# Two experts' weights loaded when the slot table is known, and a shorter piece of each zeroed row written first

## The reference

```python
x = x + layernorm(rwkv_block(layernorm(x)))      # time mixing (scans), channel mixing
xf = layernorm(x).reshape(-1, 256)
shared = (gelu(xf @ w1s) * (xf @ w2s)) @ w3s     # 256 -> 1024 -> 256
idx = argmax(xf @ Wg, axis=-1)                   # one of 8 experts for each token
for e in range(8):
    y = (gelu(xf @ W1[e]) * (xf @ W2[e])) @ W3[e]
    final = final + where(idx == e, y, 0)
out = x + layernorm(shared + final)
```

## Time and profile before

| | us |
|---|---|
| median of 3 runs | 1000.21 |
| lowest, highest | 999.18, 1000.51 |
| the profiled execution | 1001.62 |
| its span | 999.7 |
| chunk phase, to the first up matmul of slot 0 | about 664 |
| slot phase | about 336 |

### The profile page before, as it was taken

The page is one execution under the profiler, slowest core; times in us unless marked ns, Lnnn a source line. Parts: engine busy times, 40 slices in busy tenths (PEclk is TensorE's granted clock), DMA queues, the critical chain, the costliest instruction groups (busy, mean ns, idle before and its releaser), DMA issues.

```text
span 999.7 us, 27993 instructions
## 1 busy us (share of the span) xinstructions
PE 924.4 (92%) x9734; PEld 836.7 (84%) x9734; DVE 725.1 (73%) x1651; ACT 586.2 (59%) x1014; POOL 591.2 (59%) x800
## 2 busy tenths in 40 slices
PE   2477999999999999999999999869999999999994
PEld 1366888888888889888888878769999999999994
DVE  6999999999999999999999985614444444444442
ACT  5487768868868868869778755313333333333340
POOL 5475766866866866866866441434455555555553
PEclk9699999999999999999999999989999999999998
DMA  7033152152253153163171263936787778576410
GB/s 240 13 107 112 48 212 79 71 212 70 81 212 105 42 218 97 42 221 94 42 254 53 86 211 128 336 132 188 232 273 250 232 250 273 171 245 216 159 56 21
DMA packets 82091, 152.09 MB, mean 152 GB/s; under 512 B 5423, under 2 KB 62896, under 8 KB 76914
## 3 DMA queue, kind: packets, MB, share of 16 engines
q1 hardware_dynamic: 34528, 72.39, 21.1%
q10 hardware_dynamic: 42944, 61.98, 19.2%
q0 software_dynamic: 4560, 16.98, 4.4%
HBM read 183.59 MB, written 46.25 MB: 230 GB/s over the span
## 4 chain that ended last, share of the span: by engine, by line
PE 64%; DVE 11%; POOL 8%; issue 7%; ACTq 4%; DMA 3%; ACT 3%; SPq 1%; POOLq 0%; DVEq 0%
PE up L366 12%; PE up L368 12%; PE up L367 12%; PE yp L366 6%; PE yp L368 6%; PE yp L367 6%; PE yp L572 2%; PE yp L575 2%; PE tp L375 2%; ACTq L940 2%; PE yp L588 2%; DVE arena L1026 2%; POOL mix_s L1608 1%; DVE er L1127 1%; POOL routed_rows L1641 1%
## 5 line engine op out<-in xcount | busy, mean ns | idle before, releaser
L366 PE MATMUL up<-mix_s,arena 128*128 128x128 f16 x1248 | 211.9, 219 | 0.3 <-DVE ex L1474 0.2
L367 PE MATMUL up<-mix_s,arena 128*128 128x128 f16 x1248 | 211.8, 219 | 0.0
L368 PE MATMUL up<-mix_s,arena 128*128 128x128 f16 x1248 | 211.8, 219 | 0.0
L366 PE MATMUL up<-xf_s,arena 128*128 128x256 f16 x512 | 139.5, 272 | 1.5 <-issue 1.5
L1707 POOL TENSOR_TENSOR kf_s<-ex,kf_s 128x512 f16<-128x512 f32 x78 | 90.2, 1156 | 85.6 <-ACT kf_s L986 85.5
L368 PE MATMUL up<-xf_s,arena 128*128 128x256 f16 x512 | 139.5, 273 | 0.0
L367 PE MATMUL up<-xf_s,arena 128*128 128x256 f16 x512 | 139.5, 272 | 0.0
L1474 DVE SCALAR_TENSOR_TENSOR ex<-up,ex 128x512 f32<-128x512 f32 x78 | 53.9, 691 | 102.6 <-ACT ex L980 102.5
L366 PEld LDWEIGHTS up<-mix_s,arena 128*128 128x128 f16 x1248 | 122.4, 98 | 1.3 <-DVE ex L1474 1.2
L367 PEld LDWEIGHTS up<-mix_s,arena 128*128 128x128 f16 x1248 | 122.4, 98 | 0.4
L368 PEld LDWEIGHTS up<-mix_s,arena 128*128 128x128 f16 x1248 | 122.4, 98 | 0.0
(11 more groups left out here) (226 smaller groups left out, 2865.6 us busy)
## 6 DMA issues: line engine op xcount, KB each, us to landing
arena<-w_split ACTq DMA_DIRECT2D x113, 1024.0 KB
arena<-in_W SPq DMA_DIRECT2D x24, 1024.0 KB, 6.5
w_split<-arena SPq DMA_DIRECT2D x24, 1024.0 KB, 9.2
rows<-routed_rows ACTq DMA_DIRECT2D x39, 261.0 KB, 2.8
arena<-w_split SPq DMA_DIRECT2D x9, 1024.0 KB
normed<-routed_rows ACTq DMA_DIRECT2D x37, 128.0 KB, 2.5
x_in<-in_x SPq DMA_DIRECT2D x16, 256.0 KB, 2.8
x_res<-in_x SPq DMA_DIRECT2D x16, 256.0 KB, 2.8
```

What stands on the lines that cost most here:

```text
L366: pe.matmul(out, stat(0), mov(0), start=first, stop=False)
L367: pe.matmul(out, stat(0), mov(1), start=False, stop=False)
L368: return pe.matmul(out, stat(1), mov(0), start=False, stop=last)
```

## The change

The prefetch is taken out. The up weights of slots 0 and 1 are loaded by SP once the table names their experts, slot 0's ahead of its x, and slot 1's between the two loads of x. The down piece of slot 0 is loaded by ACT, without a condition. Ahead of the first x only the last 260 numbers of each zeroed row are written (ID to ROW), for all 8 experts by SP; the first 520 follow after slot 1's x, under a semaphore of their own, which ACT waits for ahead of its first load of a slot's rest. ACT issues no zeros. The tile of zeros shrinks from 780 to 520 numbers.

```diff
@@ -120,7 +120,7 @@
         x2 = sb("x2", tok)
         gate_r = sb("gate_r", tok)
         relu_k = [sb(f"relu_k{b}", chan) for b in range(2)]
-        zero_row = ex.rearrange("p n k c -> p (n k c)")[:, 2 * CT * CH:2 * CT * CH + ROW]
+        zero_row = ex.rearrange("p n k c -> p (n k c)")[:, 2 * CT * CH:2 * CT * CH + ID]
         mixed2 = relu_k
         kf_s = sb("kf_s", [2, FT, CH], F16)
         kf = kf_s.rearrange("p h f n -> p (h f n)").bitcast(F32).rearrange("p (f n) -> p f n", f=FT)
@@ -296,9 +296,15 @@
 
                 sp.wait_ge(S("end_at"), 1)
                 sp.wait_ge(S("zero_row"), 1)
-                for e in range(E // 2):
+                for e in range(E):
                     at = sp.value_load(end_at[0:1, e:e + 1], min_val=0, max_val=E * REGION - P)
-                    sp.dma_start(routed_rows[bass.ds(at, P)], zero_row).then_inc(S("zeroed"), 16)
+                    sp.dma_start(routed_rows[bass.ds(at, P), ID:ROW], zero_row[:, 0:ROW - ID]).then_inc(S("zeroed"), 16)
+
+            def other_zeros_at_ends():
+
+                for e in range(E):
+                    at = sp.value_load(end_at[0:1, e:e + 1], min_val=0, max_val=E * REGION - P)
+                    sp.dma_start(routed_rows[bass.ds(at, P), 0:ID], zero_row).then_inc(S("zeroed_rest"), 16)
 
             def half(w, part):
                 return w.rearrange("p m h (k n) -> p (m h k) n", k=CT)[:, :, part * F // 2:(part + 1) * F // 2]
@@ -306,37 +312,24 @@
             def up_halves(e, part):
                 return half(w_split[bass.ds(e, 1), :, 0:2].rearrange("e p m h n -> (e p) m h n"), part)
 
-            def likely_slots():
-
-                sp.wait_ge(S("scattered1"), 16 * TT * (NC // 2 - 1))
+            def first_slots():
+
+                sp.wait_ge(S("slot_table"), 2)
                 for m in range(3):
                     sp.wait_ge(S(f"expert_lo{m}"), E)
-                    sp.wait_ge(S(f"expert_out{m}"), 16 * (E - 1))
-                for part in range(2):
-                    sp.dma_start(half(expert_w[0][:, 0:2], part),
-                                 half(w_split[0, :, 0:2], part)).then_inc(S(f"slot_w{part}_0"), 16)
-                sp.dma_start(expert_w[0][:, 2], w_split[0, :, 2]).then_inc(S("slot_w2_0"), 16)
-                for m in range(3):
                     sp.wait_ge(S(f"expert_out{m}"), 16 * E)
-                for part in range(2):
-                    sp.dma_start(half(expert_w[1][:, 0:2], part),
-                                 half(w_split[0, :, 0:2], part)).then_inc(S(f"slot_w{part}_1"), 16)
-
-            def first_slots():
-
-                sp.wait_ge(S("slot_table"), 2)
-                sp.wait_ge(S("scattered_xf"), 16 * TT)
-                sp.wait_ge(S("zeroed"), 16 * E)
-                for b in range(2):
-                    sp.wait_ge(S(f"scattered{b}"), 16 * TT * (NC // 2 - b))
                 for n in range(2):
+                    e = sp.value_load(slot_expert[0:1, n:n + 1], min_val=0, max_val=E - 1)
+                    for part in range(2):
+                        sp.dma_start(half(expert_w[n][:, 0:2], part),
+                                     up_halves(e, part)).then_inc(S(f"slot_w{part}_{n}"), 16)
+                    if n == 0:
+                        sp.wait_ge(S("scattered_xf"), 16 * TT)
+                        sp.wait_ge(S("zeroed"), 16 * E)
+                        for b in range(2):
+                            sp.wait_ge(S(f"scattered{b}"), 16 * TT * (NC // 2 - b))
                     at = sp.value_load(slot_row[0:1, n:n + 1], min_val=0, max_val=E * REGION - P)
                     sp.dma_start(slot_x[n], routed_rows[bass.ds(at, P), XF:XF + C]).then_inc(S(f"slot_x_in{n}"), 16)
-                    e = sp.value_load(slot_expert[0:1, n:n + 1], min_val=0, max_val=E - 1)
-                    for part in range(2):
-                        sp.wait_ge(S(f"slot_w{part}_{n}"), 16)
-                        sp.dma_start(half(expert_w[n][:, 0:2], part), up_halves(e, part),
-                                     cond=e != 0).then_inc(S(f"slot_w{part}_{n}"), 16)
 
             def step(i, p, h):
                 for part in range(2):
@@ -353,9 +346,9 @@
                 for e, m in early_piece(i, p, h) + last_late(i, p, h) + late_now(i, p, h):
                     store_expert(e, m)
                 if at_step(i, NC + 1):
-                    likely_slots()
                     zeros_at_ends()
                     first_slots()
+                    other_zeros_at_ends()
 
             chunk_steps(sp, step)
 
@@ -403,7 +396,7 @@
                 if is_slot(j):
                     wait(pe, S("slot_x_lo"), j + 1)
                     for q in range(2):
-                        wait(pe, S(f"slot_w{q}_{b}"), 16 * (h + 2))
+                        wait(pe, S(f"slot_w{q}_{b}"), 16 * (h + 1))
                         wait(pe, S("slot_g"), 2 * j + q - 1)
                         for m in range(2):
                             for g in range(FT // 2):
@@ -414,7 +407,7 @@
                                                lambda s: slot_xs[b][:, s, k, :], k == 0, k == CT - 1)
                         mm.then_inc(S("slot_up"), 1)
                 if is_slot(j - 1):
-                    wait(pe, S(f"slot_w2_{1 - b}"), 16 * (h + 2 * b))
+                    wait(pe, S(f"slot_w2_{1 - b}"), 16 * (h + b))
                     wait(pe, S("slot_h_lo"), 2 * j)
                     wait(pe, S("slot_sum"), j - 2)
                     if at_step(j, 2):
@@ -831,13 +824,6 @@
                     for n in own_pieces(OWN_HI, i, part):
                         own_hi(n)
 
-                def zeros_at_end(e):
-                    if at_step(i, NC + 1):
-                        act.wait_ge(S("end_at"), 1)
-                        act.wait_ge(S("zero_row"), 1)
-                        at = act.value_load(end_at[0:1, e:e + 1], min_val=0, max_val=E * REGION - P)
-                        act.dma_start(routed_rows[bass.ds(at, P)], zero_row).then_inc(S("zeroed"), 16)
-
                 def late_hi():
                     for e, m in late_piece(i, p, h):
                         expert_hi(e, m)
@@ -883,8 +869,6 @@
                 gelu(0)
                 if at_step(i, NC):
                     late_hi()
-                zeros_at_end(E // 2)
-                zeros_at_end(E // 2 + 1)
                 gelu(1)
                 if not at_step(i, -1):
                     ln0(i + 1, 1 - p)
@@ -904,8 +888,6 @@
                     early_hi()
                 mix_hi(0)
                 sh_hi(0)
-                zeros_at_end(E // 2 + 2)
-                zeros_at_end(E // 2 + 3)
                 if at_step(i, NC + 1):
                     gelu(2)
                 mix_hi(1)
@@ -949,9 +931,6 @@
                 fresh = None
                 if not isinstance(n, int) or n >= 2:
                     fresh = e != expert_of(n - 2)
-                if at_step(n, 0):
-                    act.wait_ge(S("slot_w2_0"), 16)
-                    fresh = e != 0
                 wait(act, S(used), value)
                 if part == 2:
                     dst, src = expert_w[b][:, 2], w_split[bass.ds(e, 1), :, 2]
@@ -988,6 +967,7 @@
                                        ACT.Copy).then_inc(S("slot_h_hi"), 1)
                     if at_step(j, 0):
                         act.wait_ge(S("scattered_rest"), 16 * TT * 2)
+                        act.wait_ge(S("zeroed_rest"), 16 * E)
                     at = rows_of(j)
                     wait(act, S("slot_done"), j - 1)
                     act.dma_start(slot_rest[b], routed_rows[at, 0:OFF + 1]).then_inc(S(f"slot_rest_in{b}"), 16)
```

## The result

Over five runs each the changed kernel took 1004.56 us (1002.68 to 1004.79) and the kernel before 999.18 (998.62 to 1000.51). The ratio is 1.0043, with a 95% interval of 1.0029 to 1.0058: slower by 4.3 us, 2.9 to 5.8 (the two medians lie 5.4 apart). The forecast was 1003.2, slower by 3.0, in a range of 1000.4 to 1006.8.

What follows compares the result with a forecast made beforehand. PE was taken to bound the kernel, so slot 0's start decides: +1.5 us for x of slot 1 and +1.5 for the clock make +3.0, 1003.2 us; the 8 in 10 range was 1000.4 to 1006.8.

Steps and rivals of the forecast that it cites:

- What bounds: PE bounds the slot phase, so time gained or lost at slot 0's first matmul reaches the end whole.
- Zeros: SP's eight short zeros before the first x take 1.12 us a turn, end at 648.1, land about 2.1 us after issue.
- the rival of SP's slow loop: SP's register reads stay slow, eight zero turns of 1.68 us end at 652.6: 1007.6 us in all, chance 0.15.
- Slot table and weights: Before slot 0: table ready at 648.2, first weight issue at 649.4, x issues near 651.6 and 656.
- x of slot 1: Behind weights in queue 1 it lands at 664.8; slot 0's matmuls start at 665.4 instead of 663.86, +1.5 us.
- Clock: PE's two gaps leave slot 0 at half speed for 4.7 us instead of 1.8, until 670.1: +1.5 us.
- The sum: Slot 0's later start and the low clock, 1.5 + 1.5 = +3.0 us, giving 1003.2 us.
- Costed at nothing: Slot 0's down weights and ACT's wait for the rest zeros add no time; the cover is 3 to 5 us.
- ACT held: Rest zeros landing as late as 678 delay ACT's gelu of slot 1 past its cover: 1005.2 us, chance 0.08.
- Faster: The x loads pass the weights in queue 1, slot 0 starts at 659.0: 994.4 us, chance 0.07.

Runs made afterwards that it cites:

- the two experiments that brought slot 0 forward: Changed kernel with x of slot 1 ahead of slot 1's weights: 1.0038; kernel before with short zeros first, prefetch kept: 0.9968.
- the other two with prefetch: Kernel before with short zeros first: 0.9968; the same plus slot 0's rest load by SP and both x issued together: 0.9975.

## Why the prediction was right, point by point

**What bounds.** Slot 0's start decides, and the rest follows: borne out by the kernels with moved orders only so far as ACT and DVE keep up. The changed kernel's delay of 2.5 us at that start and 2.9 at slot 0's end reached the end of its span as 3.1.

**Zeros.** Eight turns were to end at 648.1 and took until 648.7; the register read took 0.27 as taken, so the rival of SP's slow loop is out. The reason given was wrong, though: it put the slow reads of before down to the loaded queue, but the reads of the rest zeros, the first of them with some 2 MB ahead in SP's queue, took 0.28:

```profile
L306 SPq TENSOR_LOAD <-end_at x8: 266/277/684, 659.2 to 668.3; - x8
```

The short zeros landed 1.7 us after issue, 2.1 forecast.

**Slot table and weights.** The table was forecast for 648.2. Its last cast took 1.14 us and ended at 648.8; the first weight issue was at 649.78 (649.4 forecast). x of slot 0 was issued at 651.74 (651.6) and x of slot 1 at 656.46 (656).

**x of slot 1.** Landed near 665.7 against 664.8, and x of slot 0 near 659.3 against 657.6. The order in the queue was right. So was the rate: 4.46 MB of queue 1 from 650.7 to 664.2 are 0.33 MB/us, beside the other queues. SP's queue after, in 651 to 663, in 651 to 652 and in 659 to 665:

```profile
q1 hardware_dynamic: 3872, 3.90, 98.0%
```

```profile
q1 hardware_dynamic: 212, 0.22, 65.7%
```

```profile
q1 hardware_dynamic: 2029, 2.12, 109.0%
```

Without its first microsecond the first stretch holds 3.68 MB in 11 us, 0.335 MB/us, and the last ran at 0.353. What was mis-sized was the start. The first weights were issued 0.4 us late, and 0.22 MB are what 0.335 MB/us moves in 0.7 us, so the full rate counts from about 651.3 (an estimate from these rows) and not from 650.7. That is 0.6 of the 0.9 us by which x of slot 1 was late; the rest is not placed. The term came out at +2.5 instead of +1.5. The Trainium skill has two limits in "DMA: Bandwidth & Descriptors", section Specifications: queue 1 reaches the fabric's 435 GB/s in none of these stretches, and the 358 GB/s of HBM per core stand just above its best, 353. All queues together went beyond 358 where zeros were written beside the loads, with 399 GB/s in 666 to 667, so as a limit of everything that a core moves the trace does not bear it out.

**Clock.** Forecast +1.5; measured +0.4 in both profiles of the changed kernel and +1.7 in that of the kernel with only the rest load moved, which has the same passage. It was low at slot 0's start, as said. The forecast had it rise 5.2 us after PE's second start, as before after the only one; it rose after 3.0 and 3.1 us in the first two, so that slot 0 ran slow for 2.6 us instead of 4.7, and after 5.8 us in the third. What decides this is open, so the size of this term was within what occurs but could not be had from the one profile of before. The forecast also knows of no fall ahead of the gaps. The page "TensorE: Matmul & The Clock Gate" of the Trainium skill, section HAM oscillation, has each wait paid anew; the low clock at slot 0's start agrees with it (0.50 in 666 to 667), but the extra price in this case was 0.4 us twice and 1.7 once.

**The sum** of 3.0 met 2.9 at slot 0's end because one term was 1.0 too small and the other 1.1 too large: that is luck, and with the clock of the third profile the measured sum would have been 4.2. The measured 4.3 (2.9 to 5.8) is somewhat more; what the remainder is made of is open: two profiles of the same kernel differ by 1.8 us from end_at to the end, and slot 0's up phase alone by 1.3 where the passage is the same.

**Costed at nothing.** Slot 0's down weights: no wait. ACT's wait for the rest zeros was forecast to end at 673 and ended at 677.4. The cover that had been given for it, 3 to 5 us, was nearly used, and it held only because slot 0 itself was late; in the two experiments that brought slot 0 forward and left the wait where it was, it cost PE 3.1 and 2.2 us. The rival "ACT held" was the right mechanism with the wrong condition: it gates what brings slot 0 forward, not the change itself.

**Faster.** The x loads did not pass the weights: 7.6 and 9.2 us to landing.

## What to carry to other kernels

A load that the next work waits for belongs ahead of bulk loads in its queue: here moving one 128 KB load in front of 2.1 MB brought the start forward by 3.3 us. Shortening what a gate waits for is worth most where it stands behind other traffic (6 us of start with the prefetch, 2 without), so find what is ahead of it before deciding what to drop. And when a critical start moves forward, look at which in-order engine holds a wait that was hidden behind it; without the prefetch the gain came only when that wait was moved to an engine with nothing behind it (1.0038 to 1.0009).

## What the runs showed of the hardware that was not expected

The spread between executions begins long before the passage. In 13 profiles, all with the same work up to there, end_at was ready between 636.6 and 639.4 us. Six of them had a granted clock of 0.74 in 20 to 60 us and 0.87 in 60 to 100, and are the six at 639.0 to 639.4; of the seven with 0.96 in 60 to 100, six are at 636.6 to 638.3 and one, the kernel before, at 639.2. So a shift of some 2 us of all that follows goes with the clock of the first 100 us in 12 of 13 profiles; no run tests which causes which.

The clock also fell after short gaps and in the midst of matmuls. All 13 profiles have the same gap of 1.6 to 1.7 us in the shared down product. In six of them (the changed kernel's two among them) the clock fell within 1.1 us behind it, in seven, the kernel before among them, it did not: the length of the gap alone does not decide. In the kernel with 100 idle matmuls PE had idled 1.7 us before 651.44 and then worked without a gap, and the mean clock of 652 to 656 was 0.63. In the one with 64, PE had idled 2.0 us before 664.5, and it was 0.94 in 664 to 666 and 0.50 in 666 to 668. So filling a gap in part did not keep the clock.

SP's register reads of end_at took 0.83 us before (0.70 at least), 0.70 in the kernel with prefetch and rest load by SP, 0.52 and 0.87 in the other two with prefetch (medians of four), and 0.27 in the changed kernel, whose later reads beside a loaded queue took 0.28. In the slow cases ACT read the same tile at the same time; but in the kernel with whole zeros and SP alone the median was 0.45, so what slows them stays open.
